# A loop order with parted transposes and a hand-scheduled drain, in a fused cross-attention, sigmoid self-attention and expert kernel

## The chip, the cores and the metric

The kernel runs on one core of one Trainium2 chip. The metric is the device time of one execution in microseconds (us). Engines are named as in the profile: PE is TensorE (matmuls), PEld its weight loads, DVE VectorE, ACT ScalarE, POOL GpSimd, SP the engine that issues most DMAs.

## The reference, cut to what matters

128 sequences of 32 query rows, each with a context of 257 rows, all 256 wide. Three layers run one after the other, each with a residual:

```python
# layer 1: layernorm(x), cross-attention to the context, 16 heads of 16
scores = q @ k.T ; attn = softmax(scores) ; x1 = x + (attn @ v) @ Wo.T + bo
# layer 2: layernorm(x1), rms_norm, rotary q and k, self-attention over 32 rows
weights = sigmoid(scores / 4) ; weights /= sum(weights) + 1e-8 ; x2 = x1 + (weights @ v) @ o_w.T + o_b
# layer 3: layernorm(x2), top-1 router over 8 experts, capacity 160, in token order
expert_idx = argmax(softmax(y2 @ gate_w + gate_b)) ; pos = running count of tokens of that expert - 1
out = x2 + gate_prob * (gelu(dispatch @ w1 + b1) @ w2 + b2)      # tokens with pos < 160 only
```

## The kernel before

The 4096 rows are cut into T = 32 tiles of 128 (four sequences each, j = 0 to 3). Every engine has its own program, written out by hand in its order, and semaphores tie them together. `body(i)` is one turn of the loop. It works on three tiles at once: cross-attention of tile i (called xa), the first part of layer 2 of tile t1 = i - 1 (s1) and the rest of layer 2 and the router of tile t2 = i - 2 (s2). The loop has T + 2 = 34 turns, so the last two turns hold no cross-attention: they are the end of the pipeline (the drain) for the last two tiles. Below, A is tile 30 and Z tile 31, the last.

In a turn, PE does for each of the four sequences: `scores` (L425), a block of `keys` (L394, six matmuls of 512 columns) for a later one, `values` (L405) of the next, `transpose_probs` (L441, eight transposes in two groups c = 0, 1; each group waits for DVE's normalised probabilities of its c), and `weighted_values` (L454). The small blocks of layer 2 stand between these, in a table `between` whose key is (sequence, place): `short(j, place)` runs them.

```python
(0, 0): s2 and (lambda: (turn("relu_done", t2 + 1), scores2(t2))),
(3, 3): lambda: (s2 and (turn("logit_done", t2 + 1), gate(t2)),
                 s1 and (spare_free(xa, i, 3), project_v2(t1))),
```

All layer-2 blocks but a few share one PSUM bank, `shared`. `turn(sem, count)` makes a block wait until the reader of the bank's last contents is through. `scores2` (L501) needs the rotated queries in a block-diagonal form `qbd2`: ACT copies the transposed queries and keys to `qkT` (L701), then SP issues eight DMAs (`send_diag`, L255), one for each group of 16 partitions, and PE waits for `qbd2_in`. ACT makes tanh, relu, abs and exp of these scores (L773 to L782), DVE multiplies them to the sigmoid weights (L1028), PE multiplies by the values (`self_values`, L516), DVE divides (L1040), PE transposes and projects (L469, L463). The residual (L1049), its layernorm (L1053 to L1064, the power on POOL, L1264), transposes, `gate` (L524), `logits`, ACT's exp (L787), `choose` (DVE, L1076 to L1088: softmax, its maximum, one-hot) and `positions` (L532, L533) follow. POOL turns the position into a row number (`slot_numbers`, L1287 to L1306) and scatters the tile's rows to HBM (`send`, L1316). When all 32 sends have landed, SP loads the rows of the first experts (L331) and PE transposes them (L630): the expert stage, eight experts of L656 and L670 each. In the loop's DVE program the same pieces stand between `maxima` (L934) and `normalise` (L941, L945).

## Time and profile before

| what | us |
|---|---|
| median of 3 runs (lowest, highest) | 1164.42 (1162.83, 1166.78) |
| the profiled execution | 1167.37 |
| its span, first to last instruction | 1165.6 |
| PE busy / PEld / DVE / ACT / POOL | 1085.9 / 878.5 / 894.5 / 790.5 / 251.5 |
| last turn with cross-attention ends, PE's first block of the drain starts at | 1017.58 |
| first transpose of the expert stage starts at | 1071.85 |

The profile gives each engine's busy time and, for each group of instructions, how long the engine sat idle before it and what ended that. PE's busy time contains modelled ends of pipelined matmuls, so a block's own length also holds small waits inside it. The row PEclk gives the granted TensorE clock in tenths: 9 or more is the upper level (2.4 GHz), 5 the lower (1.2 GHz).

### The profile page before, as it was taken

How to read it: one execution, taken by the hardware profiler on the slowest of the kernel's cores; microseconds unless marked ns; L12 is line 12 of the kernel's file. 1: busy time of each engine (PE TensorE's matmuls, PEld its weight loads, DVE VectorE, ACT ScalarE, POOL GpSimd, SP SyncE). 2: the span in 40 equal slices, each digit the busy share in tenths (PEclk: the TensorE clock that was granted, in tenths of full speed). 3: DMA queues.
4: the chain of work that ended last, by engine and by line, in shares of the span. 5: the costliest groups of instructions: out<-in, count | busy, mean ns of one | idle time of the engine just before them, and what ended most of it. 6: DMA issues, size and time to landing. Idle time of an engine off the chain costs nothing. (4 is left out here: it accounts for less than half of the span.)

```text
span 1165.6 us, 40738 instructions
## 1 busy us (share of the span) xinstructions
PE 1085.9 (93%) x16137; PEld 878.5 (75%) x16137; DVE 894.5 (77%) x2655; ACT 790.5 (68%) x2313; POOL 251.5 (22%) x565
## 2 busy tenths in 40 slices
PE   5899999999999999999999999999999999853996
PEld 4678777777778777777877778877777777642996
DVE  5678788888888888888888888888888888731111
ACT  5677677777777777777777778777777777421221
POOL 0011122222222222222222222222212222222111
PEclk9899999999999999999999999999999999855999
DMA  4352422222222121221111111112211110001573
GB/s 128 113 142 72 172 65 63 65 64 57 61 61 58 45 60 55 58 53 54 43 55 57 56 58 57 57 57 58 57 44 52 52 53 17 16 11 35 180 254 105
DMA packets 71915, 82.15 MB, mean 70 GB/s; under 512 B 16987, under 2 KB 50732, under 8 KB 71728
## 3 DMA queue, kind: packets, MB, share of 16 engines
q1 hardware_dynamic: 65280, 75.19, 22.1%
q0 software_dynamic: 3200, 3.71, 0.9%
q8 instruction: 129, 2.11, 0.8%
q10 hardware_dynamic: 3248, 0.66, 0.3%
q14 instruction: 58, 0.48, 0.1%
HBM read 64.79 MB, written 16.56 MB: 70 GB/s over the span
## 5 line engine op out<-in xcount | busy, mean ns | idle before, releaser
L724 ACT ACTIVATE prob<-score,nmx 128x257 f32<-128x257 f32 x512 | 235.8, 475 | 127.1 <-DVE nmx L934 127.0
L405 PE MATMUL vps<-wv_p,ctx_p 128*128 128x256 f32 x1536 | 213.4, 289 | 0.0
L934 DVE TENSOR_REDUCE nmx<-score 128x2 f32<-128x514 f32 x256 | 165.2, 687 | 61.5 <-PE score L425 61.5
L394 PE MATMUL kps<-ctx_p,wk_p 128*128 128x512 f32 x768 | 209.5, 408 | 2.3 <-issue 1.3
L405 PEld LDWEIGHTS vps<-wv_p,ctx_p 128*128 128x128 f32 x1536 | 195.6, 192 | 4.2
L945 DVE TENSOR_SCALAR prob<-prob,rsum 128x256 f32<-128x256 f32 x512 | 164.7, 364 | 9.1
L394 PEld LDWEIGHTS kps<-ctx_p,wk_p 128*128 128x128 f32 x768 | 138.5, 191 | 42.8 <-issue 14.2
L441 PE MATMUL score<-const,prob 128*128 128x128 f32 x1024 | 150.2, 280 | 7.4 <-DVE prob L945 5.1
L1264 POOL TENSOR_TENSOR rstd<-ve,const 128x1 f32<-128x1 f32 x64 | 52.7, 823 | 480.7 <-DVE ve L988 265.7
L441 PEld LDWEIGHTS score<-const,prob 128*128 128x128 f32 x1024 | 112.1, 141 | 24.5 <-DVE prob L945 22.1
L926 DVE SCALAR_TENSOR_TENSOR ctx_p<-ctxT,nlast,ctx_p 128x256 fp32r<-128x256 f32 x256 | 111.7, 478 | 8.1 <-ACT ctx_p L741 8.1
L741 ACT ACTIVATE ctx_p<-ctxT,nlast 128x256 fp32r<-128x256 f32 x256 | 116.8, 516 | 0.8 <-issue 0.8
L732 ACT ACTIVATE kT<-kps,b_k 128x512 f32<-128x512 f32 x128 | 89.1, 696 | 24.6 <-PE kps L394 23.1
L724 ACT ACTIVATION_READ_ACCUMULATOR prob<-score,nmx 128x1 f32 x512 | 104.9, 205 | 0.0
L748 ACT ACTIVATE vv<-vps 128x512 f32<-128x512 f32 x128 | 79.2, 619 | 23.5 <-PE vps L405 23.5
L454 PE MATMUL gather<-probT,vv 128*32 128x64 f32 x4096 | 92.3, 225 | 1.8 <-DVE probT L951 0.7
L454 PEld LDWEIGHTS gather<-probT,vv 128*32 128x32 f32 x4096 | 70.5, 110 | 29.8 <-issue 22.4
L425 PE MATMUL score<-kT,qz 32*64 32x257 f32 x2048 | 89.6, 403 | 2.7 <-issue 1.6
L757 ACT ACTIVATE probT<-score 128x512 f32<-128x512 f32 x128 | 78.2, 611 | 11.3 <-PE score L441 11.2
L951 DVE COPY probT<-score 128x512 f32<-128x512 f32 x96 | 66.3, 690 | 19.6 <-PE score L441 16.6
L872 ACT ACTIVATE hid<-score,ffb 128x160 f32<-128x160 f32 x64 | 20.8, 391 | 68.1 <-PE score L656 67.1
L516 PEld LDWEIGHTS shared<-v2a,th 32*32 32x32 f32 x4096 | 44.7, 109 | 28.2 <-issue 21.6
(150 smaller groups left out, 1749.8 us busy)
## 6 DMA issues: line engine op xcount, KB each, us to landing
ctxT<-in_ctxT SPq DMA_DIRECT2D x128, 257.0 KB, 3.1
w<-in_w SPq DMA_DIRECT2D x16, 1024.0 KB, 9.1
xq<-in_x SPq DMA_DIRECT2D x32, 128.0 KB, 2.1
xr<-in_x SPq DMA_DIRECT2D x32, 128.0 KB, 2.0
qbd<-qkT SPq DMA_DIRECT2D x256, 16.0 KB, 1.8
out<-row SPq DMA_DIRECT2D x32, 128.0 KB, 3.0
slots<-row SPq DMA_DIRECT2D x10, 257.0 KB, 5.6
x_a<-slots SPq DMA_DIRECT2D x8, 129.0 KB, 2.2
```

The source lines that it names most:

```text
L394: last = mm(kps[:, :], wk_p[:, x, n, c * P:(c + 1) * P], ctx_p[:, y, n, 2 * r:2 * r + 2, :].rearrange("p j s -> p (j s)"), start=(n, x) == ...
L405: last = mm(vps[:, c, :], ctx_p[:, x, n, j, c * P:(c + 1) * P], wv_p[:, y, n, :], start=(n, x) == (0, LO), stop=(n, y) == (C - 1, LO))
L425: last = mm(score[64 * e:64 * e + 64, m, 0:S], qz[rows, half, e, j, :, :].rearrange("p h q -> p (h q)"), kT[rows, j // 2, e, j % 2, :], st ...
L441: last = nc.tensor.transpose(score[:, 2 * c, at:at + P], prob[:, 2 * c + g, n * P:(n + 1) * P], k["ident"])
L454: last = mm(gather[32 * g:32 * g + 32, c, :, j * L:(j + 1) * L], vv[:, b_slot(j), n, c * P + 32 * g:c * P + 32 * g + 32], probT[:, c, n, 2 ...
L724: last = af(prob[:, m, :], score[:, m, 0:S], ACT.Exp, bias=nmx[:, m:m + 1], scale=1.0, accum_out=esum[:, m:m + 1])
L732: af(kT[:, r, c, :, 0:SM], kps[:, :].rearrange("p (j s) -> p j s", j=2), ACT.Identity, bias=b_k[:, c:c + 1], scale=1.0).then_inc(s["k_evac ...
L741: last = af(ctx_p[:, HI, c, j, :], ctxT[:, r, c, j % 2, 0:SM], ACT.Identity, bias=nlast[:, c, b:b + 1], scale=1.0)
L748: af(vv[:, j % 2], vps[:, :, :], ACT.Copy).then_inc(s["v_evac"], 1)
L926: last = v.scalar_tensor_tensor(ctx_p[:, LO, c, j, :], ctxT[:, r, c, j % 2, 0:SM], nlast[:, c, b:b + 1], ctx_p[:, HI, c, j, :].bitcast(F32 ...
L934: v.tensor_reduce(nmx[:, 2 * c:2 * c + 2], score[:, 2 * c:2 * c + 2, 0:S], AX.X, ALU.max, negate=True).then_inc(s["max_done"], 1)
L945: last = v.tensor_scalar(prob[:, m, 0:SM], prob[:, m, 0:SM], rsum[:, m:m + 1], None, ALU.mult)
```

## The change

Four things change.

1. **Loop order on PE.** `scores2` moves from place (0, 0) to (0, 1), behind the block of keys. `transpose_probs` is parted into its two groups, with a new place between them (place 3; the old place 3 is now 4). Between the groups stands for j = 0 the first of the six matmuls of the keys block of j = 1 (which keeps five), and for j = 3 the first two of the six matmuls of `project_v2`; its other four and then `gate` follow the second group.
2. **Routing.** `choose` compares the logits with their maximum instead of the softmax with its own; the gate's weight is the reciprocal of the sum of exps (`gate_weight`). The slot arithmetic drops a running counter.
3. **The drain.** The loop ends after 32 turns, and `drain()` on each engine is written out for tiles A and Z. Tile A uses the bank `kps`, Z uses `shared`; the query blocks of Z are made by eight copies of 32 partitions (six on ACT, two on DVE) straight from PSUM instead of ACT's copy and eight DMAs; the rotation goes in halves (queries, then keys); the sigmoid's relu and abs are on DVE, and the tanh goes in halves; slots of A and Z are computed on DVE; Z has a row buffer of its own.
4. **Holds.** `hold(n)` issues n matmuls of 512 columns whose result nobody reads, at eight places of PE's drain, 12+5+2+4+5+1+3+24 = 56 in all.

```diff
+BUILD = 6
+HOLDS = (12, 5, 2, 4, 5, 1, 3, 24)
...
+        A, Z = T - 2, T - 1
+        half_c = score[:, 2, 0:C * P].rearrange("p (c n) -> p c n", c=C)
+        last_c = vps[:, 0, :].rearrange("p (c n) -> p c n", c=C)
+        halves2 = shared[:, 0:D], score[:, 2, 0:D]
+        chunks = vps[:, 0, 0:P], spare[:, 0:P]
+        row_z, x1b_z = ctxT[:, 0, 0].rearrange("p j s -> p (j s)"), ctxT[:, 0, 1, 0, 0:D]
 
...
-                    (0, 0): s2 and (lambda: (turn("relu_done", t2 + 1), scores2(t2))),
+                    (0, 1): s2 and (lambda: (turn("relu_done", t2 + 1), scores2(t2))),
                     (0, 2): once(i) and (lambda: (turn("vlast_done", C), last_rows())),
-                    (0, 3): lambda: (s1 and (turn("x1_step", 3 * t1 + 1),
-                                             project_out(att, wo, "ext_step", 2 * t1 + 2, t1, "o1_ps"))),
+                    (0, 3): xa and (lambda: keys(i, 1, 1, 0, 1)),
...
-                    (3, 3): lambda: (s2 and (turn("logit_done", t2 + 1), gate(t2)),
-                                     s1 and (spare_free(xa, i, 3), project_v2(t1))),
+                    (3, 3): s1 and (lambda: (spare_free(xa, i, 3), project_v2(t1, 0, 2))),
+                    (3, 4): lambda: (s1 and project_v2(t1, 2, 6), s2 and (turn("logit_done", t2 + 1), gate(t2))),
                 }
...
-                        transpose_probs(i, j)
+                        transpose_probs(i, j, 0)
                     short(j, 3)
                     if xa:
+                        transpose_probs(i, j, 1)
+                    short(j, 4)
+                    if xa:
                         weighted_values(i, j)
 
...
+            def hold(n):
+
+                for _ in range(n):
+                    mm(score[:, 0, :], wk_p[:, HI, 0, 0:P], aqk_p[:, HI, 0, :], start=True, stop=True)
+
+            def drain():
+
+                turn("relu_done", A + 1, "kps")
+                scores2(A, kps)
+                transpose_biases()
+                pe.wait_ge(s["pta_evac"], B)
+                pe.wait_ge(s["ptb_evac"], B)
+                turn("x1_step", 3 * Z + 1)
+                project_out(att, wo, "ext_step", 2 * Z + 2, "o1_ps")
+                positions(A - 1)
+                hold(HOLDS[0])
+                pe.wait_ge(s["v2_done"], A + 1)
+                transpose_rows(y1, "y1_done", Z, "y1t_ps", spare_c)
+                self_values(A, range(0, 6), kps, "kps")
+                turn("qk_done", Z + 2)
+                project_qk(Z)
+                self_values(A, range(6, 11), kps, "kps")
+                hold(HOLDS[1])
+                transpose_half(0, half_c, Z + 1)
+                self_values(A, range(11, H), kps, "kps")
+                project_v2(Z, 0, 6)
+                turn("qkT_done", Z + 1)
+                transpose_half(C, sh_c, Z + 2)
+                hold(HOLDS[2])
+                turn("relu_done", Z + 2)
+                pe.wait_ge(s["qbd_act"], BUILD)
+                pe.wait_ge(s["qbd_dve"], HH - BUILD)
+                for c in range(C):
+                    for j in range(TB):
+                        last = mm(halves2[c][32 * j:32 * j + 32, :], qkT[:, C + c, 32 * j:32 * j + 32],
+                                  qbd2[:, c, :, 32 * j:32 * j + 32], start=True, stop=True)
+                last.then_inc(s["s2_ps"], 1)
+                transpose_rows(att2n, "att2n_done", A, "at2_ps", last_c)
+                hold(HOLDS[3])
+                turn("x2_step", 3 * A + 1, "kps")
+                project_out(att2, ao, "att2_done", A + 1, "o2_ps", kps)
+                self_values(Z, range(0, 8), ends=(7, H - 1))
+                self_values(Z, range(8, H), score[:, 2, :])
+                transpose_chunk(att2n, 0, "att2n_done", Z + 1, chunks[0], "at2_ps")
+                transpose_rows(row, "y2_done", A, "y2t_ps", spare2_c)
+                transpose_chunk(att2n, 1, "att2n_done", Z + 2, chunks[1], "at2_ps")
+                turn("x2_step", 3 * Z + 1)
+                for c in range(C):
+                    pe.wait_ge(s["att2_done"], Z + 1 + c)
+                    last = mm(shared[:, 0:D], att2[:, c, :], ao[:, c, :], start=c == 0, stop=c == C - 1)
+                last.then_inc(s["o2_ps"], 1)
+                turn("logit_done", A + 1, "kps")
+                gate(A, kps)
+                hold(HOLDS[4])
+                transpose_rows(row_z, "y2_done", Z, "y2t_ps", spare_c)
+                positions(A)
+                hold(HOLDS[5])
+                turn("logit_done", Z + 1)
+                gate(Z)
+                hold(HOLDS[6])
+                pe.wait_ge(s["cum_read"], Z)
+                positions(Z)
+                hold(HOLDS[7])
 
             tiles(body)
-            transpose_biases()
...
+            def query_blocks():
+
+                act.wait_ge(s["qkt_ps"], Z + 1)
+                act.wait_ge(s["s2_ps"], A + 1)
+                for h in range(BUILD):
+                    r = slice(32 * (h // 2), 32 * (h // 2) + 32)
+                    af(qbd2[r, :, h, :], half_c[r], ACT.Copy, scale=k["odd" if h % 2 else "even"][r]
+                       ).then_inc(s["qbd_act"], 1)
+
+            def copy_chunk(dst, src, ready, count, done):
...
+                query_blocks()
...
+                dve.wait_ge(s["route_step"], 4 * t + 1)
+                v.tensor_reduce(lm[:, :], logit[:, :], AX.X, ALU.max).then_inc(s["route_step"], 1)
...
-                dve.wait_ge(s["ex_done"], t + 1)
-                v.reciprocal(rse[:, :], se[:, :]).then_inc(s["route_step"], 1)
-                dve.wait_ge(s["route_step"], 5 * t + 2)
-                v.tensor_scalar(pr[:, :], ex[:, :], rse[:, 0:1], None, ALU.mult).then_inc(s["route_step"], 1)
-                dve.wait_ge(s["route_step"], 5 * t + 3)
-                v.tensor_reduce(row[:, 2 * D:2 * D + 1], pr[:, :], AX.X, ALU.max).then_inc(s["route_step"], 1)
-                dve.wait_ge(s["route_step"], 5 * t + 4)
-                v.scalar_tensor_tensor(eqr[:, :], pr[:, :], row[:, 2 * D:2 * D + 1], k["rank"], ALU.is_equal, ALU.mult
+                dve.wait_ge(s["route_step"], 4 * t + 2)
+                v.scalar_tensor_tensor(eqr[:, :], logit[:, :], lm[:, 0:1], k["rank"], ALU.is_equal, ALU.mult
                                        ).then_inc(s["route_step"], 1)
-                dve.wait_ge(s["route_step"], 5 * t + 5)
...
+
+            def gate_weight(t, row=row):
+                dve.wait_ge(s["ex_done"], t + 1)
+                v.reciprocal(row[:, 2 * D:2 * D + 1], se[:, :]).then_inc(s["route_step"], 1)
...
+                residual_bias(Z)
+                power("1", "x1_done", Z + 1, Z, "x1_pow")
+                slot_numbers(A - 1)
+                rms(Z)
+                pool.wait_ge(s["ctx_parts"], B)
+                g.tensor_tensor(x1b_z, x1[:, :], r_o2[:, :], ALU.add).then_inc(s["x1b_done"], 1)
+                send(A - 1)
+                power("2", "x2_done", A + 1, A, "x2_pow")
+                power("2", "x2_done", Z + 1, Z, "x2_pow")
+                pool.wait_ge(s["sloti_done"], 6)
+                send(A, sloti_a)
+                pool.wait_ge(s["sloti_done"], 12)
+                send(Z, sloti_z, row_z)
+
             tiles(body)
-            slot_numbers(T - 1)
```

The order of PE's instructions in one turn, at the end of sequence 3, before. Names are out<-in of the matmul: `prob` is the probabilities (transposes), `y2T` the gate's input, `y1T_p` that of project_v2.

```order
L469 MATMUL score<-const,row 128x128 x2
L441 MATMUL score<-const,prob 128x128 x8
L524 MATMUL shared<-gw,y2T 128x8 x2
L486 MATMUL score<-av_p,y1T_p 128x256 x6
L454 MATMUL gather<-probT,vv 32x2x32 x16
```

The same place in the changed kernel:

```order
L483 MATMUL score<-const,row 128x128 x2
L455 MATMUL score<-const,prob 128x128 x4
L500 MATMUL score<-av_p,y1T_p 128x256 x2
L455 MATMUL score<-const,prob 128x128 x4
L500 MATMUL score<-av_p,y1T_p 128x256 x4
L539 MATMUL shared<-gw,y2T 128x8 x2
L468 MATMUL gather<-probT,vv 32x2x32 x16
```

The eight transposes are now four and four with two value matmuls between, and the gate stands last. The start of the next turn before, from the scores of sequence 0 to the output projection (`wo`) of the tile in layer 2:

```order
L425 MATMUL score<-kT,qz 64x257 x8
L501 MATMUL shared<-qbd,qkT 32x256 x8
L394 MATMUL kps<-ctx_p,wk_p 128x512 x6
L405 MATMUL vps<-wv_p,ctx_p 128x256 x12
L441 MATMUL score<-const,prob 128x128 x8
L463 MATMUL shared<-wo,att 128x256 x2
```

and in the changed kernel:

```order
L441 MATMUL score<-kT,qz 64x257 x8
L409 MATMUL kps<-ctx_p,wk_p 128x512 x6
L516 MATMUL shared<-qbd,qkT 32x256 x8
L421 MATMUL vps<-wv_p,ctx_p 128x256 x12
L455 MATMUL score<-const,prob 128x128 x4
L409 MATMUL kps<-ctx_p,wk_p 128x512
L455 MATMUL score<-const,prob 128x128 x4
L477 MATMUL shared<-wo,att 128x256 x2
```

The query-block matmuls (`qbd`) moved behind the keys, and one keys matmul stands between the groups of transposes. The third place is PE's program for the last tile, from its self-attention scores to the projection, before:

```order
L501 MATMUL shared<-qbd,qkT 32x256 x8
L516 MATMUL shared<-v2a,th 32x17 x44
L532 MATMUL score<-oh,tri_bf 128x8
L533 MATMUL score<-seen,ones_bf 128x8
L516 MATMUL shared<-v2a,th 32x17 x20
L469 MATMUL score<-const,att2n 128x128 x2
L463 MATMUL shared<-ao,att 128x256 x2
L469 MATMUL score<-const,row 128x128 x2
L524 MATMUL shared<-gw,y2T 128x8 x2
L612 MATMUL kps<-const,ffb_rows 128x80
```

and in the changed kernel (L646 is `hold`; `row` belongs to tile A):

```order
L636 MATMUL shared<-const,qk 128x128 x2
L646 MATMUL score<-aqk_p,wk_p 128x512 x2
L677 MATMUL shared<-qbd,qkT 32x256 x4
L677 MATMUL score<-qbd,qkT 32x256 x4
L483 MATMUL vps<-const,att2n 128x128 x2
L646 MATMUL score<-aqk_p,wk_p 128x512 x4
L477 MATMUL kps<-ao,att 128x256 x2
L531 MATMUL shared<-v2a,th 32x17 x32
L531 MATMUL score<-v2a,th 32x17 x32
L641 MATMUL vps<-const,att2n 128x128
L483 MATMUL score<-const,row 128x128 x2
L641 MATMUL score<-const,att2n 128x128
```

What moved: the last tile's scores (L677) go to two banks, tile A's transposes and projection (`att2n`, `ao`) and two holds stand between the last tile's blocks, and its values (L531) come in two halves, each in a bank of its own.

## Rows read from the trace of the kernel before

**Rows 1.** The page: span, busy time, PE's granted clock in 40 slices.

```profile
span 1165.6 us, 40738 instructions
...
PE 1085.9 (93%) x16137; PEld 878.5 (75%) x16137; DVE 894.5 (77%) x2655; ACT 790.5 (68%) x2313; POOL 251.5 (22%) x565
...
PEclk9899999999999999999999999999999999855999
```

**Rows 2.** Waits of PE, 100 to 1000 us: total, times, longest.

```profile
PE shared L501 <- DMA qbd<-qkT: 12.6, 13, 1.4
```

**Rows 3.** Waits of PE's weight loads, 100 to 1000 us.

```profile
PEld score L441 <- DVE prob L945: 15.8, 58, 0.7
```

**Rows 4.** Line L463: durations ns, first and last start us.

```profile
L463 PE MATMUL shared<-wo,att x128: 379/379/483, 58.7 to 1021.5; 128*128 128x256 f32 x128
```

**Rows 5.** Timeline of PE, one turn: start, length, instructions, idle before.

```profile
504.03 1.65 PE L478 MATMUL shared<-aqk_p,y1T_p 128*128 128x512 f32 x6
...
508.56 1.03 PE L441 MATMUL score<-const,prob 128*128 128x128 f32 x8
...
516.05 1.29 PE L441 MATMUL score<-const,prob 128*128 128x128 f32 x8
...
517.63 0.96 PE L486 MATMUL score<-av_p,y1T_p 128*128 128x256 f32 x6
...
520.76 1.07 PE L501 MATMUL shared<-qbd,qkT 128*32 128x256 f32 x16 [0.87 <-DMA qbd<-qkT]
521.76 1.65 PE L394 MATMUL kps<-ctx_p,wk_p 128*128 128x512 f32 x6
...
532.43 1.26 PE L441 MATMUL score<-const,prob 128*128 128x128 f32 x8
```

**Rows 6.** Timeline of DVE around choose, the same turn.

```profile
525.93 0.15 DVE L1076 RECIPROCAL rse<-se 128x1 f32<-128x1 f32 x1
...
527.18 0.42 DVE L977 TENSOR_TENSOR x<-shared,xr 128x256 f32<-128x256 f32 x1
```

**Rows 7.** Timeline of PE, last turn with cross-attention to experts.

```profile
1011.92 0.41 PE L469 MATMUL score<-const,row 128*128 128x128 f32 x2 [3.29 <-DVE row L1064]
...
1017.58 1.96 PE L501 MATMUL shared<-qbd,qkT 128*32 128x256 f32 x16
1020.72 1.13 PE L463 MATMUL shared<-wo,att 128*128 128x256 f32 x4 [1.18 <-ACT sneg L774]
...
1027.77 2.93 PE L478 MATMUL shared<-aqk_p,y1T_p 128*128 128x512 f32 x6 [1.06 <-DVE att2n L1040]
...
1042.52 1.93 PE L501 MATMUL shared<-qbd,qkT 128*32 128x256 f32 x16 [1.98 <-DMA qbd<-qkT]
1047.45 1.37 PE L516 MATMUL shared<-v2a,th 32*32 32x17 f32 x88 [3.00 <-issue]
...
1063.26 0.19 PE L532 MATMUL score<-oh,tri_bf 128*128 128x8 bf16 x1 [2.04 <-DVE oh L1088]
...
1071.85 0.45 PE L630 MATMUL shared<-const,y_a 128*128 128x128 f32 x1 [8.38 <-issue]
...
1073.83 6.69 PE L656 MATMUL score<-disp,w 128*128 128x160 f32 x32 [0.64 <-DVE disp L1223]
...
1087.69 2.88 PE L656 MATMUL score<-disp,w 128*128 128x160 f32 x20
```

**Rows 8.** Timeline of ACT in the drain.

```profile
1037.53 0.38 ACT L701 ACTIVATE y2T<-score 128x256 f32<-128x256 f32 x1 [1.41 <-PE score L469]
...
1044.51 0.60 ACT L773 ACTIVATE th<-shared 128x512 f32<-128x512 f32 x1 [4.62 <-PE shared L501]
```

**Rows 9.** Timeline of DVE in the drain.

```profile
1056.17 0.42 DVE L1049 TENSOR_TENSOR row<-shared,x1b 128x256 f32<-128x256 f32 x1 [3.45 <-PE shared L463]
```

**Rows 10.** Timeline of SP in the drain.

```profile
1036.15 5.03 SPq L255 DMA_DIRECT2D qbd<-qkT  x8
```

**Rows 11.** Timeline of POOL, the last send.

```profile
1067.01 1.12 POOL L1316 DMA_INDIRECT slots<-row,sloti  x1 [0.87 <-issue]
```

348 lines of the change are left out of this document (253 added, 95 removed).

## The prediction, made before the changed kernel ran

> **What bounds the kernel now.** I read the page first: PE is busy 1085.9 of the span's 1165.6 us, the next engine (DVE) 894.5 [rows 1]. In the clock line the reader sees 9 in nearly all slices and 5 in the two slices from about 1020 to 1078 us: the drain runs at the lower clock. So there are two stages with different limits. In the loop PE is the bound. Line L463 with `wo` runs once per tile, from 58.7 to 1021.5 us over 32 tiles [rows 4]: (1021.5 - 58.7) / 31 = 31.06 us a tile. What PE still waits for there: 12.6 us in 13 tiles for the DMAs of the query blocks [rows 2], and its weight loads stand 15.8 us in 58 places, two a tile, for the probabilities [rows 3]. The latter hides in block lengths: eight transposes take 1.03 us for sequence 2, but 1.29 and 1.26 us for sequences 3 and 1, so 0.26 and 0.23 us of standing a tile [rows 5]. In the drain nothing is full: from 1017.58 to 1071.85 us, 54.3 us, one tile's chain sets the end, with each block waiting for DVE, ACT, SP or POOL [rows 7].
>
> **The loop, part by part.** *scores2 behind the keys.* In the turn shown the block waits 0.87 us for its DMAs [rows 5], at worst 1.4 [rows 2]. The keys block ahead of it now takes about 1.5 us (six matmuls, 1.65 us with the last one's end, rows 5), so the wait is covered. Behind scores2 on PE came keys and values, which need nothing of it; ACT's tanh stood behind the evacuation of the keys already. I take 12.6 x 32 / 29 = about 13 us (31 turns at most have it). What is late next: the output projection needs ACT's relu; between the end of scores2 and it lie still the values and the transposes, about 2.6 us, against two ACT passes of 0.60 us [rows 8]. Covered.
>
> *Parted transposes.* For sequence 3 two of six value matmuls (0.96 us the block, 0.32 for two) [rows 5] cover the 0.26 us. For sequence 0 the first keys matmul, 1.65 / 6 = 0.27 us, is taken out of sequence 1, whose transposes then come 0.27 us earlier and would stand 0.23 + 0.27 = 0.50 us. Against that stands the shorter `choose`: six small DVE instructions and their waits take 1.25 us (525.93 to 527.18) [rows 6], now four, so about 0.83; DVE reaches the maxima of sequence 1 0.4 us earlier. Net, sequence 1 stands 0.1. So 0.26 + 0.13 = 0.39 us a tile plus what sequence 0 stood (bounds 0 and 0.25). Each cut also changes twice between kinds of matmul, of which no row shows a price alone; bounds are 0 and the 0.27 us of a whole matmul. I take 0.3 us a tile net, 31 x 0.3 = 9 us; bounds: -4 us (nothing is gained at sequence 0 and 1, and changes cost 0.13 a tile) and +15 (0.49 x 31).
>
> The loop gives 13 + 9 = 22 us, bounds 9 and 28. The rest of the routing change (DVE and POOL instructions) is off PE's path: DVE has 23% free [rows 1].
>
> **The drain.** I go along the chain by its marks on PE [rows 7] and lay the new order beside it, at the upper clock.
> - Start to projection `wo`: 3.14 us before (1017.58 to 1020.72, it waited for the relu of the same bank); now tile A's scores are in another bank and only the two extracts gate it: 1.7. Gain 1.4.
> - To the qk projection: 7.05 us (to 1027.77; tile A's values and division stood in the bank); now x1, norm, power, transpose, two copies: 5.4. Gain 1.6.
> - To the query-block scores: 14.75 us (to 1042.52). In it are the projection at 2.93 us (1.65 at the upper clock, rows 5), tile A's projection in the bank, the ACT copy of 0.60 and the DMAs, 5.03 us of issue on SP [rows 10] and landing. Now: 1.7 the projection, 3.3 the rotation in halves, 0.45 the last transposes, 0.45 the DVE copy of the key half (the price of 128x256, 0.42 [rows 9]). The six ACT copies run beside the second half: 32 x 256 is in no row, bounded by nothing and by a 128x256 copy, 0.38 [rows 8]; six are at most 2.3 us against 2.1 of cover. Sum 5.9. Gain 8.8.
> - To the self values: 4.93 us (to 1047.45) against 4.6 now: no abs and exp on one engine in a row, but the tanh in halves waits for relus. Gain 0.3.
> - To the residual row: 8.72 us (to 1056.17 on DVE [rows 9]); it held 88 matmuls, one more wait, the division, transpose, copy and a projection at the lower clock. Now in halves beside each other: 4.6. Gain 4.1.
> - To the last positions: 7.09 us (to 1063.26), now 5.6: transposes and gate at the upper clock, ACT's exp off the chain. Gain 1.5.
> - To the first expert transpose: 8.59 us (to 1071.85). Seven POOL instructions become three DVE ones, and the send of 1.12 us after 0.87 of issue [rows 11] stays: 7.4. Gain 1.2.
>
> Sum 18.9, so 35.4 us. These "now" figures add same-kind instructions and assume no hold is late. A hold matmul has 512 columns, 1.65 / 6 = 0.27 us at the upper clock and 2.93 / 6 = 0.49 at the lower [rows 5, 7]. The last 24 are 6.6 us against 7.4 of waiting: hidden. The first 12 are 3.3 us against 2.6: 0.6 late. At the lower clock they are 5.9, 3.3 late, and the last 24 are 11.7, 4.3 late.
>
> **The clock.** Before, PE waited 3.29 us at 1011.92 [rows 7] and the page's clock line falls behind it. That wait is in the last cross-attention turn and stays, so the drain starts partly at the lower clock; then 12 holds follow without a pause. I take 2.5 us for blocks and holds before it is back at the upper level: drain 38, gain 16 (bounds 6, all of it at the lower clock, which I add up to 48 us; and 19). The Trainium skill ("TensorE: Matmul & The Clock Gate", section "What's actually happening") says that the throttled clock is the default and that activity releases it. By that rule the holds bring the upper level and the drain is the 38 us; had I gone by the row alone, in which a drain of scattered blocks, six full matmuls of 2.93 us among them, stayed at 5 tenths to its end, it would be 48.
>
> ACT's small copies have a second price: the skill's "ScalarE: Activation LUTs", "Rules for kernel authors", budgets about 0.3 us per instruction and 0.83 ns per element, 0.51 us for 256 against the 0.38 of the row. By it six copies would be 3.1 us and the scores 1 us later.
>
> **The expert stage.** Its first block of 32 matmuls takes 6.69 us partly at the lower clock [rows 7]; a later one is 20 in 2.88 us, so 32 are 4.5. With the holds ahead it starts at the upper clock: gain 2.2, and 0.3 of the transposes; 2.5 (0 if the clock is low). Nothing else in it changes.
>
> **Sum.** 22 + 16 + 2.5 = 40.5: span 1165.6 - 40.5 = 1125. The profiled execution took 1167.37, 1.8 over its span, and was 2.95 above the median 1164.42. So the median becomes 1164.4 - 40.5 = 1124.
>
> **The rivals.**
> - *The waits move instead of going* (chance 0.20). The parted transposes give nothing: sequence 1's wait grows by the key matmul taken from it, and the switching eats the rest. For it: 0.27 us taken away there against 0.4 from DVE is a thin margin. Against: sequence 3 has only gain. The loop then gives 13 or less: 1124 + 9 + up to 4 = 1133 to 1137.
> - *The holds are late* (0.15). The clock stays low in the drain; each hold block is then longer than the wait it fills, the last by 4.3 us, and the expert stage starts low. Drain 48: 1124 + 10 + 2.5 = 1136. For it: rows 1 show two slices at 5. Against: no block before had 12 matmuls of 512 columns.
> - *All waits go* (0.13). The loop gives 28 and the drain 19: 1124 - 6 - 3 = 1115.
> - *Slower than before* (0.03). The first keys matmul of sequence 1 now waits between the transposes for ACT's evacuation of sequence 0's keys, which stands behind four exps; before, a block of scores lay between. If the evacuation ended late, PE would stand in every tile with the second group of transposes, the projection and the next scores behind it. I see it done about 1 us ahead. To turn 40 us into a loss it would have to cost 40.5 / 31 = 1.3 us a tile, so be 2.3 us late: 1168 at 1.4.
> - *The forecast* (0.48), within 1119 to 1130.
>
> Within 0.3% (3.5 us, about what a measurement of this kernel can tell from no change) needs a loss of the same kind that just offsets; 0.01. Faster 0.96, slower 0.03. Range: from the "all waits go" case to both large rivals, 1112 to 1137.
>
> **What would show it.** Right: no row of PE waiting for the qbd DMAs in the loop; `wo` once in 30.3 to 30.5 us; the transposes of sequence 3 as 4 and 4 with no standing between; PE's first expert transpose some 38 us after the last weighted values; the clock line with at most one slice below 9 there. Wrong: a new wait of PE for ACT's `kT` or `sneg` in the loop; the weight loads of the transposes standing as long as before; holds that end after the data they wait beside; a 5 in the clock line in the drain.

## The result, and the profile of the changed kernel

| | median us | lowest, highest | runs |
|---|---|---|---|
| before | 1165.12 | 1162.83, 1166.78 | 4 |
| changed | 1118.60 | 1116.88, 1122.84 | 4 |

The ratio is 0.9603, with a 95% interval of 0.9582 to 0.9624: 46.5 us less, where 40.5 were forecast. The forecast of 1124 is 5.4 us above the median, and the median lies in the range. The profiled execution took 1118.18 us.

The page of the changed kernel first, against [rows 1]: span, busy times, clock.

```profile
span 1116.0 us, 40828 instructions
...
PE 1076.0 (96%) x16193; PEld 878.4 (79%) x16193; DVE 878.8 (79%) x2649; ACT 798.5 (72%) x2318; POOL 242.4 (22%) x516
...
PEclk9899999999999999999999999999999999989998
```

PE's busy time fell by 10 us only, the span by 50. In the new busy time are 15.7 us of the 56 hold matmuls, which do no work for the result, so some 26 us of real blocks went too (what they stood inside their lengths, and the lower clock), and PE's idle time went from 79.7 to 40.0 us. In the clock line the slices 8, 5, 5 of before have become a single 8, with another 8 in the last slice. The next views answer to [rows 2] (PE's waits, 100 to 950 us, because the loop ends earlier now), [rows 3] (its weight loads, the same stretch), [rows 4] (the output projection with `wo`, line L463 before and L477 now) and, further down, [rows 5]. The waits of PE, the waits of the weight loads:

```profile
PE shared L516 <- DMA qbd<-qkT: 1.0, 3, 0.6
```

```profile
PEld score L455 <- DVE prob L1076: 0.4, 2, 0.2
```

Both waits of the loop are nearly gone. Over the same 100 to 950 us the kernel before has 12.6 us, now 1.0, and 14.2 us for the weight loads (15.8 over the longer stretch of [rows 3]), now 0.4. The row of `wo` by its line:

```profile
L477 PE MATMUL shared<-wo,att x128: 379/379/454, 58.3 to 992.4; 128*128 128x256 f32 x128
```

From the first to the last `wo` there were 962.8 us, in turns of 31.06; now there are 934.1, in turns of 30.13. Next is PE's timeline over one seam of two turns (start, length, instructions, idle before in brackets). L455 is `transpose_probs`, L500 `project_v2`, L409 `keys`, L516 `scores2`.

```profile
532.56 0.60 PE L455 MATMUL score<-const,prob 128*128 128x128 f32 x4
532.92 0.49 PE L500 MATMUL score<-av_p,y1T_p 128*128 128x256 f32 x2
533.24 0.61 PE L455 MATMUL score<-const,prob 128*128 128x128 f32 x4
533.62 0.73 PE L500 MATMUL score<-av_p,y1T_p 128*128 128x256 f32 x4
...
535.24 0.69 PE L441 MATMUL score<-kT,qz 32*64 32x257 f32 x16
535.86 1.66 PE L409 MATMUL kps<-ctx_p,wk_p 128*128 128x512 f32 x6
537.45 1.07 PE L516 MATMUL shared<-qbd,qkT 128*32 128x256 f32 x16
...
539.98 0.60 PE L455 MATMUL score<-const,prob 128*128 128x128 f32 x4
540.34 0.48 PE L409 MATMUL kps<-ctx_p,wk_p 128*128 128x512 f32 x1
540.66 0.60 PE L455 MATMUL score<-const,prob 128*128 128x128 f32 x4
541.09 1.03 PE L477 MATMUL shared<-wo,att 128*128 128x256 f32 x4
```

Two value matmuls stand between the groups of transposes of sequence 3, and one keys matmul between those of sequence 0. A row's length holds a modelled end, so I read from start to start. From the first transpose of sequence 3 to the next scores it is 535.24 - 532.56 = 2.68 us. In the turn of [rows 5] the transposes began at 516.05 and the next scores at 519.20, so the same blocks took 3.15. That is 0.47 us a turn, but not by the parting alone: in these blocks the gate has moved too, from ahead of the value matmuls to behind them. From the scores of sequence 0 to `wo` it is now 541.09 - 535.24 = 5.85 us. To compare, here is PE's timeline of *before* in a turn without a wait for DMAs:

```profile
395.29 0.69 PE L425 MATMUL score<-kT,qz 32*64 32x257 f32 x16
...
399.85 1.36 PE L441 MATMUL score<-const,prob 128*128 128x128 f32 x8
401.04 1.03 PE L463 MATMUL shared<-wo,att 128*128 128x256 f32 x4
```

That was 401.04 - 395.29 = 5.75 us. Here the transposes of sequence 0 took 1.36 us, so they stood 0.33 us more than the 1.03 of an unhindered group, which I had bounded by 0 and 0.25. In the turns in which PE waited for the DMAs they took 1.03. The whole trace of before bears this out: from start to start these transposes take 0.87 or 0.88 us in all 13 turns of the window with a DMA wait, and 1.19 to 1.21 in 13 of the 14 without (1.00 in the long turn with the loads). The two waits took turns: DVE caught up while PE stood for the DMAs. So one keys matmul more before `wo` costs 0.10 us there, and the block that gave it away is 0.23 us shorter (1.56 to 1.33): together 0.60 us a turn.

The drain, PE's timeline against [rows 7]. L646 is `hold`, L492 the qk projection, L677 the last tile's scores, L531 its values, L547 `positions`, L722 and L748 the expert stage.

```profile
984.56 0.66 PE L483 MATMUL score<-const,row 128*128 128x128 f32 x2 [3.29 <-DVE row L1198]
...
990.15 1.36 PE L516 MATMUL kps<-qbd,qkT 128*32 128x256 f32 x16
...
991.65 1.10 PE L477 MATMUL shared<-wo,att 128*128 128x256 f32 x4
...
997.25 1.62 PE L492 MATMUL shared<-aqk_p,y1T_p 128*128 128x512 f32 x6 [0.50 <-DVE y1T_p L1128]
...
1004.06 0.64 PE L677 MATMUL shared<-qbd,qkT 128*32 128x256 f32 x8 [0.42 <-DVE qkT L1383]
...
1007.87 0.69 PE L531 MATMUL shared<-v2a,th 32*32 32x17 f32 x62 [0.31 <-issue]
...
1018.27 0.17 PE L547 MATMUL score<-oh,tri_bf 128*128 128x8 bf16 x1 [0.45 <-issue]
...
1018.32 5.84 PE L646 MATMUL score<-aqk_p,wk_p 128*128 128x512 f32 x24
1024.88 0.30 PE L722 MATMUL shared<-const,y_a 128*128 128x128 f32 x1 [0.71 <-issue]
...
1026.42 4.61 PE L748 MATMUL score<-disp,w 128*128 128x160 f32 x32 [0.64 <-DVE disp L1486]
```

The drain, from its first block to the first expert transpose, took 54.3 us and takes 34.7. The wait of 3.29 us at the row's transposes is still there, to the hundredth, and the view of windows (PE busy, ..., then the granted clock PEclk) shows what follows it:

```profile
984.00:992.00 8.00, 7.20 (x71) 6.02 (x72) 4.97 (x17) 1.79 (x5) 0.99 (x2) 0.58 0.11 29
992.00:1000.00 8.00, 7.36 (x117) 5.44 (x116) 4.12 (x15) 2.62 (x8) 4.43 (x13) 1.00 0.01 3
...
1012.00:1016.00 4.00, 3.81 (x14) 2.69 (x14) 2.53 (x13) 0.48 (x3) 0.55 (x1) 0.67 0.10 33
```

PEclk is 0.58 in the eight microseconds around and behind the wait. By finer windows it is 0.50 from 984 and back at the upper level at about 990.8, before the first hold starts at 992.64. The projection at 997.25 takes 1.62 us, the upper level's price; before it took 2.93 in the same place. The clock is lower only once more in the drain, from about 1011.3 to 1014.3 (0.67 in the window 1012 to 1016). The expert stage's first 32 matmuls take 4.61 us where they took 6.69.

### The profile page after: what moved, and what is told of

Its sections match the earlier page's. It is cut to its first block, busy times and chain, and to the rows that moved or that the text cites. A ratio compares the mean times of both kernels' runs of the same rounds, so it can differ in the third digit from the quotient of the medians.

```text
span 1116.0 us, 40828 instructions
## 1 busy us (share of the span) xinstructions
PE 1076.0 (96%) x16193; PEld 878.4 (79%) x16193; DVE 878.8 (79%) x2649; ACT 798.5 (72%) x2318; POOL 242.4 (22%) x516
## 4 chain that ended last, share of the span: by engine, by line
PE 84%; issue 4%; DVE 3%; DMA 3%; SPq 2%; POOL 1%; ACT 1%; POOLq 0%; DVEq 0%; ACTq 0%
PE vps L421 16%; PE kps L409 15%; PE score L455 9%; PE score L441 7%; PE gather L468 6%; PE shared L477 5%; PE shared L492 4%; PE shared L531 4%; PE score L762 3%; PE shared L516 3%; PE score L748 3%; PE shared L398 2%; PE score L483 2%; PE score L500 2%; PE shared L508 2%
## 5 line engine op out<-in xcount | busy, mean ns | idle before, releaser
L409 PE MATMUL kps<-ctx_p,wk_p 128*128 128x512 f32 x768 | 217.9, 412 | 1.9 <-issue 1.0
L421 PE MATMUL vps<-wv_p,ctx_p 128*128 128x256 f32 x1536 | 216.5, 291 | 0.0
L421 PEld LDWEIGHTS vps<-wv_p,ctx_p 128*128 128x128 f32 x1536 | 193.0, 191 | 14.0 <-issue 12.4
L409 PEld LDWEIGHTS kps<-ctx_p,wk_p 128*128 128x128 f32 x768 | 138.6, 191 | 40.4 <-issue 14.8
L1076 DVE TENSOR_SCALAR prob<-prob,rsum 128x256 f32<-128x256 f32 x512 | 159.2, 354 | 9.1
L455 PE MATMUL score<-const,prob 128*128 128x128 f32 x1024 | 147.5, 277 | 4.8 <-DVE prob L1076 4.5
L455 PEld LDWEIGHTS score<-const,prob 128*128 128x128 f32 x1024 | 115.6, 142 | 8.9 <-DVE prob L1076 7.5
L531 PEld LDWEIGHTS shared<-v2a,th 32*32 32x32 f32 x3904 | 41.3, 106 | 21.2 <-issue 17.2
```

Source lines behind the costliest of these rows:

```text
L409: last = mm(kps[:, :], wk_p[:, x, n, c * P:(c + 1) * P], ctx_p[:, y, n, 2 * r:2 * r + 2, :].rearrange("p j s -> p (j s)"), start=(n, x) == ...
L421: last = mm(vps[:, c, :], ctx_p[:, x, n, j, c * P:(c + 1) * P], wv_p[:, y, n, :], start=(n, x) == (0, LO), stop=(n, y) == (C - 1, LO))
L455: last = nc.tensor.transpose(score[:, 2 * c, at:at + P], prob[:, 2 * c + g, n * P:(n + 1) * P], k["ident"])
L531: last = mm(to[rows, h * (HD + 1):(h + 1) * (HD + 1)], th[rows, h * L:(h + 1) * L], v2a[rows, h, :], start=True, stop=True)
L1076: last = v.tensor_scalar(prob[:, m, 0:SM], prob[:, m, 0:SM], rsum[:, m:m + 1], None, ALU.mult)
```

## The experiments

All times are medians. Kernels that ran on one chip share its runs of the kernel before: 1165.65 for those without holds, with scores2 first, with whole transposes and with the loop order alone; 1166.40 for those with only the value matmuls parted, the long choose, the blocks by DMA and the holds in the last turn; 1164.71 for the last four. Across chips I compare ratios; the changed kernel had 0.9603 and, run again, 0.9614.

**Without holds.** Do the 56 holds do anything?

```diff
-HOLDS = (12, 5, 2, 4, 5, 1, 3, 24)
+HOLDS = (0, 0, 0, 0, 0, 0, 0, 0)
```

> The changed kernel with all 56 hold matmuls taken out and nothing else. Theory (the holds keep the array at the upper clock and cost nothing themselves): the drain's blocks run at the lower clock, from the last weighted values to the first expert transpose about 41 us instead of 34.7, and the first expert block about 2 us longer: 1127 us against 1118.6. Rival (the drain is short because of its order alone; the clock adds little, since its blocks are small and wait for other engines): within 2 us of 1118.6, with the clock line low or not.

Measured: 1128.54, ratio 0.9688 (0.9671 to 0.9704). Its clock line and PE's timeline in the drain:

```profile
PEclk9999999999999999999999999999999999965999
```

```profile
997.82 2.90 PE L492 MATMUL shared<-aqk_p,y1T_p 128*128 128x512 f32 x6 [0.40 <-DVE y1T_p L1128]
...
1031.01 0.45 PE L722 MATMUL shared<-const,y_a 128*128 128x128 f32 x1 [6.44 <-DMA y_b<-slots]
...
1032.98 7.06 PE L748 MATMUL score<-disp,w 128*128 128x160 f32 x32 [0.64 <-DVE disp L1486]
```

The projection takes 2.90 us again, and the experts' first block 7.06 instead of 4.61. From `wo` to the first expert transpose it is 38.8 us against 33.2. PE idles 6.44 us before that transpose, where 24 holds ended 0.71 us ahead of the data. The holds buy about 10 us by the medians. In the two traces 5.6 of it lies in the drain and 2.6 behind it. The level did come back without them: it is at the upper one from about 990.2 us, and falls at about 997.0, behind 3 us in which PE idles, to stay low until 1038. So the holds keep the level; they don't bring it back. The rest of the new drain is worth more than they are (38.8 us without them, 51.1 before).

**scores2 first again.** The loop's DMA wait by itself.

```diff
-                    (0, 1): s2 and (lambda: (turn("relu_done", t2 + 1), scores2(t2))),
+                    (0, 0): s2 and (lambda: (turn("relu_done", t2 + 1), scores2(t2))),
```

> The changed kernel with scores2 back in place (0, 0), ahead of the keys; the parted transposes stay. Theory (the move hides the DMAs of the query blocks): PE waits for them again in about half the tiles, 12 to 15 us in all, 1131 us; the shortest tile stays at 30.07 us. Rival (the DMAs would now be in time anyway, since other things moved): 1119.

Measured: 1143.34 (1138.72 to 1148.87), ratio 0.9818 (0.9777 to 0.9859). PE's waits, 100 to 950 us:

```profile
PE shared L516 <- DMA qbd<-qkT: 19.4, 15, 1.8
```

The direction is right, and the size was missed by half. Undone in the new loop, the step costs 25 us by the medians (its four runs spread over 10 us) and 20.2 in the trace from the first to the last `wo`, not 12 to 15. Some 7 of them stand in the two turns in which the expert weights load (37.6 and 33.2 us against 33.2 and 30.1), and a turn of that kind varies by itself, as shown further down. For the rest, PE now arrives 0.4 us earlier at the block (7.8 us behind the transposes that start the DMAs' chain, 8.2 before) while the DMAs land as before, so the wait grows to 19.4 us in 15 turns. And no standing elsewhere is saved by it, since the parted transposes have none left to save. In the turns without a wait, scores2 first is even 0.1 us better (29.97 to 30.07).

**Whole transposes.** Both partings taken out, scores2 left behind the keys.

```diff
-                    (0, 3): xa and (lambda: keys(i, 1, 1, 0, 1)),
...
-                    (3, 3): s1 and (lambda: (spare_free(xa, i, 3), project_v2(t1, 0, 2))),
-                    (3, 4): lambda: (s1 and project_v2(t1, 2, 6), s2 and (turn("logit_done", t2 + 1), gate(t2))),
+                    (3, 4): lambda: (s1 and (spare_free(xa, i, 3), project_v2(t1, 0, 6)), s2 and (turn("logit_done", t2 + 1), gate(t2))),
```

> The changed kernel with the eight transposes in one piece in every sequence: the keys matmul goes back to sequence 1 and the two value matmuls behind the transposes. Theory (the pieces cover the wait for the second group of probabilities): the shortest tile goes from 30.07 to about 30.5 us, 1118.6 + 12 to 15 = 1131 to 1134. Rival (the shorter choose brought the loop's 0.6 us a tile, and parting gives nothing): 1119 to 1122.

Measured: 1130.74, ratio 0.9692 (0.9676 to 0.9708), a turn of 30.43 us against 30.07. The weight loads' wait is back:

```profile
PEld score L455 <- DVE prob L1074: 11.8, 54, 0.3
```

The partings together are worth 12 us by the medians, 10.4 by the ratios and 10.2 from the first to the last `wo`: the lower end of what was expected. Sequence 3 in this kernel, with whole transposes and the gate last:

```profile
509.27 1.29 PE L455 MATMUL score<-const,prob 128*128 128x128 f32 x8
...
512.18 0.69 PE L441 MATMUL score<-kT,qz 32*64 32x257 f32 x16
```

These blocks take 2.91 us, against 3.15 before and 2.68 in the changed kernel. So the parting is worth 0.23 of the 0.47 there, and the other 0.24 is there without it.

**Only the value matmuls parted.** The key matmul goes back, the two value matmuls stay.

```diff
-                    (0, 3): xa and (lambda: keys(i, 1, 1, 0, 1)),
...
-                        keys(*((i, 1) if j < 2 else (i + 1, 0)), j % 2, lo=1 if j == 1 else 0)
+                        keys(*((i, 1) if j < 2 else (i + 1, 0)), j % 2)
```

> The changed kernel with the keys matmul back in sequence 1, so that only the transposes of sequence 3 are parted (by two value matmuls). Theory (sequence 3 holds most of what parting gives, 0.26 of the 0.36 us a tile that whole transposes cost): the shortest tile about 30.15 us, 1121 to 1122 us against 1118.6. Rival (the keys matmul gives nothing, because what it covers in sequence 0 it uncovers in sequence 1): 1118.6 or a little less. Rival (both pieces give the same): 1124.

Measured: 1123.43, ratio 0.963 (0.9604 to 0.9656), a turn of 30.20. The interval overlaps the changed kernel's (0.9582 to 0.9624), so the time alone tells nothing; the turns of the traces do. The parting at sequence 0 is worth 0.13 us a turn and that at sequence 3 the other 0.23.

**Loop order alone.** The kernel before, with the new order of PE's loop (and the DVE line that it needs: `evac_v2` ahead of `logits`); old routing, old drain. The edits are those of the first part of the diff above.

```diff
-                    (0, 0): s2 and (lambda: (turn("relu_done", t2 + 1), scores2(t2))),
+                    (0, 1): s2 and (lambda: (turn("relu_done", t2 + 1), scores2(t2))),
+                    (0, 3): xa and (lambda: keys(i, 1, 1, 0, 1)),
+                    (3, 3): s1 and (lambda: (spare_free(xa, i, 3), project_v2(t1, 0, 2))),
```

> The kernel before with PE's new loop order alone (scores2 behind the keys, parted transposes, gate last, and DVE's read of the values ahead of the logits); its choose, its drain in turns 32 and 33 and no holds. Theory (the shorter choose is needed, because sequence 1's transposes come 0.27 us earlier and were already standing 0.23): the loop gains about 17 instead of 28, 1148 us, with PE's weight loads standing for the probabilities of sequence 1 by 0.4 to 0.5 us a tile. Rival (the order alone does it): 1137.

Measured: 1143.44, ratio 0.98 (0.9781 to 0.9818): 22 us of the 46, with turns of 30.20. The weight loads still wait once a turn:

```profile
PEld score L441 <- DVE prob L950: 5.9, 28, 0.3
```

So the loop's order brings 22 us, the drain and the shorter routing the other 24. The result lies between the two theories: from the first to the last `wo` the order alone gives 21.3 of 28.6 us. Of the other 7.3 the shorter `choose` has 0.13 us a turn, the new drain's first blocks 1.2 in the last turn, and 2.5 are the turn with the loads (35.7 against 33.2), which varies by itself. Its sequence 3 takes the changed kernel's 2.67 us with the old `choose`, so no part of the 0.47 there comes from the routing.

**A long choose.** The three instructions that the change took out of `choose` (reciprocal, product and maximum of the softmax) are run again in front of it; their results are read by nobody.

```diff
+                dve.wait_ge(s["ex_done"], t + 1)
+                v.reciprocal(rse[:, :], se[:, :]).then_inc(s["pos_step"], 1)
+                dve.wait_ge(s["pos_step"], 3 * t + 1)
+                v.tensor_scalar(pr[:, :], ex[:, :], rse[:, 0:1], None, ALU.mult).then_inc(s["pos_step"], 1)
+                dve.wait_ge(s["pos_step"], 3 * t + 2)
+                v.tensor_reduce(prm[:, :], pr[:, :], AX.X, ALU.max).then_inc(s["pos_step"], 1)
+                dve.wait_ge(s["pos_step"], 3 * t + 3)
                 dve.wait_ge(s["route_step"], 4 * t + 2)
```

> The changed kernel with three more small DVE instructions in choose (reciprocal of the sum, the product with the exps, its maximum, written to tiles that nobody reads), in a chain as in the kernel before; the choice itself is unchanged. Theory (DVE reaches the maxima of sequence 1 later, and PE's transposes there stand for it): 0.15 to 0.2 us a tile, 1123 to 1125 us. Rival (the chain lies in time that DVE has free): 1119.

Measured: 1126.31, ratio 0.9642 (0.9616 to 0.9667), most turns 30.20 to 30.28.

```profile
PEld score L456 <- DVE prob L1077: 7.5, 27, 0.3
```

DVE has more than 20% free and its three small instructions cost PE 0.15 to 0.19 us a turn all the same, because the maxima of sequence 1 stand behind them and PE's second group of transposes waits for those. It is the loop-only kernel's wait again, in about as many places.

**Query blocks by DMA.** The new drain, but the last tile's blocks made as before: one ACT copy and eight DMAs.

```diff
+            sp.wait_ge(s["qbd_act"], 1)
+            sp.wait_ge(s["s2_ps"], A + 1)
+            send_diag(lambda h: qkT[HD * h:HD * (h + 1), 0:C, :], lambda h: qbd2[HD * h:HD * (h + 1), :, h, :], "qbd2_in")
...
-                pe.wait_ge(s["qbd_act"], BUILD)
-                pe.wait_ge(s["qbd_dve"], HH - BUILD)
+                pe.wait_ge(s["qbd2_in"], 16 * HH * T)
```

> The changed kernel with the last tile's query blocks made as in the loop: ACT copies the transposed queries, SP issues eight DMAs, and the eight small copies go. Theory: copy 0.4, issue 5.0, landing 1.8 us in place of about 2: the last tile's scores come 5 to 6 us later, 1124 us, and if the clock falls in the longer wait, 1126. Rival (tile A's chain would have set the end anyway): 1119 to 1120.

Measured: 1127.05, ratio 0.9661 (0.9637 to 0.9684).

```profile
1007.64 1.08 PE L680 MATMUL shared<-qbd,qkT 128*32 128x256 f32 x8 [5.29 <-DMA qbd<-qkT]
```

PE waits 5.29 us for the DMAs. From `wo` to the first expert transpose it is 39.2 us against 33.2: the copies are worth 6 us, the blocks at a lower clock behind the wait included (PEclk 0.59 and 0.56 in the windows 1004 to 1008 and 1008 to 1012).

**Holds in the last turn.** The 3.29 us wait of [rows 7] is filled too, with 12 matmuls where the next tile's query projection would stand.

```diff
-                    (3, 1): q and (lambda: (turn("qT_done", i + 2), project_queries(i + 1))),
+                    (3, 1): (q and (lambda: (turn("qT_done", i + 2), project_queries(i + 1)))) or (xa and not q and (lambda: (pe.wait_ge(s["k_evac"], C * B // 2), hold(12, kps)))),
```

> The changed kernel with 12 more hold matmuls, in the last turn with cross-attention, sequence 3, where PE waits 3.29 us for tile 29's normalised rows; they write the bank kps, whose keys are through. Theory (that wait is what drops the clock for the 6.8 us that follow, and 12 holds of 0.25 us fill it): the clock line has no fall there and the blocks from 984.6 to 990.8 us take some 2 us less, 1116.5 us. Rival (the clock falls all the same, or the holds end after the rows are there): 1118.6 to 1120.

Measured: 1119.37, ratio 0.9593 (0.9566 to 0.9619), so no difference from the changed kernel that the intervals can tell. PE's timeline, and its clock in a window of the drain:

```profile
981.74 3.03 PE L646 MATMUL kps<-aqk_p,wk_p 128*128 128x512 f32 x12
985.28 0.41 PE L483 MATMUL score<-const,row 128*128 128x128 f32 x2 [0.51 <-DVE row L1198]
```

```profile
1008.00:1012.00 4.00, 3.51 (x12) 2.56 (x12) 1.59 (x6) 0.83 (x3) 0.31 (x1) 0.60 0.12 37
```

The wait is 0.51 us, the clock stays up there, and the last turn takes 25.0 us instead of 27.16 (26.49 in a second trace of the changed kernel). But the clock falls at 1008.8 us, behind the self values, and again at 1025.9, in the experts' first block, and in this trace what was gained is lost. That the new holds moved the fall is not shown. The second trace of the changed kernel, without them, has the same fall at the same distance from the last `wo`, here its clock:

```profile
1012.00:1016.00 4.00, 3.18 (x11) 2.32 (x11) 1.55 (x7) 0.83 (x3) 0.47 (x1) 0.66 0.12 37
1016.00:1020.00 4.00, 4.00 (x14) 2.78 (x14) 3.27 (x20) 0.78 (x3) 0.55 (x1) 0.50 0.10 33
```

It falls 18.9 us behind the last `wo` there, for 6.8 us, and 18.5 us behind it with the 12 holds; in the first trace of the changed kernel it was 19.6, and for 3.1 us only. So the falls of one and the same drain differ from execution to execution, and one trace can't say what moved them.

**Gate first.** The gate ahead of the four value matmuls, with the readers' order turned as well.

```diff
-                    (3, 4): lambda: (s1 and project_v2(t1, 2, 6), s2 and (turn("logit_done", t2 + 1), gate(t2))),
+                    (3, 4): lambda: (s2 and (turn("logit_done", t2 + 1), gate(t2)), s1 and project_v2(t1, 2, 6)),
```

> The changed kernel with the gate ahead of the last four value matmuls instead of behind them, and DVE's logits ahead of its read of the values, as in the kernel before. Theory (the gate's place matters only by what PE's next block follows: the weighted values come after 0.62 us of block behind a gate and 0.68 behind value matmuls): 0.06 us a tile, 2 us in all. Rival (the read of the values comes late and the next turn's scores wait for it): 0.2 us a tile, 6 us.

Measured: 1129.10, ratio 0.9698 (0.968 to 0.9716), turns of 30.40: 0.33 us a turn lost. By the medians on this chip that is 9.4 us, more than either theory has. From start to start the second group of transposes, the value matmuls and the weighted values are 0.09, 0.09 and 0.16 us longer. The gate, then the weight loads of the next scores, then DVE's read of the values:

```profile
509.68 0.58 PE L539 MATMUL shared<-gw,y2T 128*128 128x8 f32 x4
...
511.52 0.27 PEld L441 LDWEIGHTS score<-kT,qz 32*64 32x64 f32 x16 [0.22 <-issue]
```

```profile
510.99 0.41 DVE L1152 TENSOR_TENSOR v2a<-score,r_v 128x256 f32<-128x256 f32 x1
```

The 0.16 behind the weighted values is the rival's mechanism. The next scores wait for the read of the values (`v2_done`), which DVE ends at 511.40, and their weight loads start 0.12 us after that, having stood 0.22 us. The profile puts this under "issue"; the row has 28 such places, 8.6 us from 100 to 950, where the changed kernel has 3 (2.7 us). In the changed kernel the read ends at 535.07 and the scores start at 535.24, without standing. The other 0.18 us a turn lie in blocks next to the gate; whether its place alone costs them is open.

**The changed kernel again**, on the chip of the last four.

> The changed kernel once more, unaltered, as the measure for the other kernels of this group on the same chip: 1118 to 1120 us, the loop from the first to the last projection wo 932 to 934 us in its profile.

Measured: 1119.73 (1116.60 to 1122.82), ratio 0.9614 (0.9592 to 0.9636). From the first to the last `wo` it is 935.2 us, a little over what was expected, with 3.5 us more in the turn with the loads.

**Expert loads spread.** In turn i = 2, SP issues the loads of all expert weights at once. PE's timeline of the changed kernel around the slow turn (L477 is `wo`, once a turn):

```profile
116.67 1.03 PE L477 MATMUL shared<-wo,att 128*128 128x256 f32 x4
...
128.71 0.69 PE L441 MATMUL score<-kT,qz 32*64 32x257 f32 x15 [2.02 <-issue]
...
149.90 0.38 PE L477 MATMUL shared<-wo,att 128*128 128x256 f32 x1
```

From `wo` to `wo` this turn takes 33.23 us, one with no loads 30.07; in the second trace of the same kernel it takes 36.74. The edit issues them in five parts in turns 4 to 8.

```diff
-                if once(i, 2):
-                    load_experts()
+                if 4 <= i <= 8:
+                    load_experts(i - 4)
```

> The changed kernel with the four 1 MB loads of the first experts' weights and the two bias loads spread over turns 4 to 8 instead of all in turn 2. Theory (the one turn that takes 33 us instead of 30, and its variation from run to run, come from these loads in the DMA queues): that turn takes 30.1 to 30.5 us and the time is 2.5 to 3 us lower than the changed kernel's, with less spread. Rival (that turn is long for another reason, such as code that is read in late): no change.

Measured: 1113.95 (1112.56 to 1117.72), ratio 0.9577 (0.9559 to 0.9596), 5.8 us below the changed kernel on the same chip, twice what was expected; the two intervals just touch. PE's timeline at the same place:

```profile
116.67 1.03 PE L481 MATMUL shared<-wo,att 128*128 128x256 f32 x4
...
146.73 1.03 PE L481 MATMUL shared<-wo,att 128*128 128x256 f32 x4
```

The turn takes 30.06 us, and no later one grew by more than 0.2. The long turn differs by 3.5 us between two traces of one kernel, whose times differ by 4.6, so it makes part of the spread between executions. It doesn't make all of it: with the loads spread the five runs still lie 5.2 us apart, those of the changed kernel 6.2.

**Spread loads and fuller holds together.** Spread loads, the 12 holds in the last turn, 2 holds behind the last self values (where the clock had fallen in the run with 12 holds) and 26 last ones instead of 24.

```diff
-HOLDS = (12, 5, 2, 4, 5, 1, 3, 24)
+HOLDS = (12, 5, 2, 4, 5, 1, 3, 26, 2)
...
                 self_values(Z, range(8, H), score[:, 2, :])
+                hold(HOLDS[8])
```

> The spread loads, the 12 holds in the last turn with cross-attention, two holds more behind the last tile's values and 26 instead of 24 at the end. Theory (each gives what it gave or promised alone: 3, 2 and, where the clock fell in the drain or at the experts' start, 1 to 2 us): 5 to 6 us below the changed kernel. Rival (the clock falls at other places instead): 3 us, from the loads alone.

Measured: 1111.54 (1111.07 to 1112.44), ratio 0.9547 (0.9533 to 0.9562).

```profile
span 1110.2 us, 40860 instructions
...
PEclk9899999999999999999999999999999999999999
```

Its page has no low slice in the clock line at the end, and PEclk is 1.00 in every window of its drain. This is the fastest kernel of the study: 8.2 us below the changed kernel on the same chip, where 5 to 6 were expected, and below every run of it. Its runs lie within 1.4 us, those of the changed kernel within 6.2. Against the spread loads alone it is 2.4 us; what each of the three groups of holds gives of that was not taken apart.

## Why the prediction was right, point by point

**Three stages, three sizes.** The turns gave 28.6 us from the first to the last `wo` (962.0 to 933.4 by the starts in the timelines). The last `wo` lies 3.14 us inside the drain before and 1.50 after, so 1.6 of this belongs to the drain, and the loop gave 27.0 where 22 were forecast. The drain gave 19.6 where 16 were, the expert stage with the end 2.6 where 2.5 were, and the time before the first `wo` 0.5. The sum is 49.6, rounding apart, the difference of the spans (1165.6 - 1116.0). Of the two profiled executions that of before was 2.3 us over its median and that of the changed kernel 0.4 under, so the medians differ by 46.5. The stages and their mechanisms were the right ones; two terms were too small, and one step of the loop had no term. That the median came within 5.4 us is in part luck: by the spans the forecast is 9 us short, and the profiled run of before lay 2.3 us over its median. The working also has two small slips: 12.6 x 32 / 29 is 13.9 and not 13, and the "now" figures of the drain add up to 35.2, not 35.4.

**The step that was mis-sized: the parted transposes, "0.3 us a tile net, 9 us".** The shortest turn went from 30.67 to 30.06 us, so 0.6 a turn, 18 us over 30 turns. Two pieces of it were wrong. Sequence 0 stood 0.33 us where I had bounded it by 0.25; in the turn of [rows 5] PE had just waited for DMAs, and there it doesn't stand. And sequence 3 gained 0.47 where 0.26 was foreseen. The parting gives 0.23 of that, close to the forecast. The other 0.24 is there with whole transposes too, and with the old `choose`: what is left is that the gate now stands behind the value matmuls and DVE reads the values first. The prediction had no term for this step. Undone in the new kernel, it costs 0.33 a turn, the parting 0.36 (10 to 12 us) and the shorter `choose` 0.15 to 0.19. These add up to more than the 0.61, so they overlap: what a step costs when it alone is undone is not what it gave when it was put in.

**The DMA wait, "about 13 us".** It gave less. In the 27 turns from the fourth to the thirtieth, what the turns took beyond the shortest was 11.5 us before and 3.0 after: 8.5. While PE waited for the DMAs it saved its wait for the probabilities, 0.33 us in each of 13 turns, so adding up rows of waits counts 4.3 us twice; 12.6 less 4.3 is 8.3. Taken out of the *new* kernel, the same step costs 16.3 us over the same 27 turns, 3.1 of them in the turn behind the loads. So the step is worth more there, where no other wait hides part of it. The 8.5 is worked out from the turns: no run moves scores2 alone in the kernel before. By turns: 27 x 0.61 = 16.5, plus 8.5, plus 2.0 in the first three and the last, is the 27.0.

**The loop's mark, `wo` once in 30.3 to 30.5 us**, was 30.13, on the good side.

**The drain.** By its marks, now against foreseen: to `wo` 1.5 (1.7), to the qk projection 5.6 (5.4), to the scores 6.8 (5.9), to the self values 3.8 (4.6), to the positions 10.4 (10.2), to the first expert transpose 6.6 (7.4). The sum is 34.7, where the working at full clock had 35.4. It is the 2.5 us added for a clock that starts low that failed: the clock was up again at 990.8, before the holds began, and the 12 holds end at 995.68, when DVE's rows are just done (995.67), so the transposes behind them begin at 995.82 without being late. The one piece that came out long is the scores. PE waited 0.42 us there, for DVE's copy of the key half. That copy starts at 1003.58, behind DVE's own two query-block copies (0.90 us, in no term of the working), and the rotation in halves took 3.7 us where 3.3 were foreseen. ACT's six small copies took 2.52 us together, over the 2.3 of the bound, and end at 1003.88, 0.12 us ahead of DVE's copy. By the budget in "ScalarE: Activation LUTs", section "Rules for kernel authors", of the Trainium skill the estimate for those copies was 3.1 us, which would have made the scores late; the measured 2.52 decides, and no wait for ACT stands in this trace.

**The clock.** The rival "the holds are late" (drain 48) fell, and so did the reading of the row of before alone. That the holds are the cause is shown by their removal: 38.8 us from `wo` on and a lower level over 41 us. But they act otherwise than the working had it, which let them bring the upper level. It was back before the first hold, with holds and without; they kept it from falling at 997. The throttled level as the default that activity releases, as "TensorE: Matmul & The Clock Gate", section "What's actually happening", in the Trainium skill has it, agrees with the trace: without holds PEclk is 0.50 from 1000 to 1032 us, with them 1.00 in most windows. But the refilled drain is not safe: in the traces of kernels with these holds the level mostly still falls, for 3 to 7 us at a time, and not at the same times in two traces of the same kernel. Only the trace with spread loads and fuller holds has no fall at all.

**The rivals in the loop.** "The waits move" fell: the weight loads' wait went from 14.2 to 0.4 us over the same stretch. "Slower", by a late evacuation of keys, showed no wait at all. "All waits go" (28 and 19, so 1115, chance 0.13) came nearest, to the measured 27.0 in the loop and 19.6 in the drain; its 49.5 us in all are what the spans show. By the median, 1118.6 lies between it and the forecast, 3.6 us from the one and 5.4 from the other.

## What to carry to other kernels

Where two waits alternate in a loop, read each one in the turns in which the other is absent: sums over all turns count one twice and hide the other, and the same reordering then has two prices (8.5 us put in, 16 us taken out, over the same 27 turns). An engine with a fifth of its time free can still set the pace by where a small instruction stands in its queue, so look at what is behind it. When a chain at the end of a kernel leaves the array idle, filler matmuls that end before their neighbour's data cost nothing and keep the clock from falling (10 us here), but take more than one trace before you say where it still falls. And give every block that a change moves a term in the sum, the small ones too: the gate's two matmuls, moved back together with DVE's order, cost 0.33 us a turn.
